# Graph attention on one core: gaps in SBUF that set how the operands of the matmuls lie modulo 256

## The reference

```python
def gat_layer(x, W, a_s, a_d, b, edge_index, concat):
    h = (x @ W).reshape(n, H, C)
    alpha_s = einsum('nhc,hc->nh', h, a_s); alpha_d = einsum('nhc,hc->nh', h, a_d)
    e = leaky_relu(alpha_s[src] + alpha_d[dst], 0.2)
    e = exp(e - segment_max(e, dst)[dst])
    alpha = e / (segment_sum(e, dst)[dst] + 1e-16)
    return segment_sum(h[src] * alpha[:, :, None], dst).reshape(n, H * C) + b
h = elu(gat_layer(x, W1, a_src1, a_dst1, b1, edges, True))       # 8 heads of 768
out = gat_layer(h, W2, a_src2, a_dst2, b2, edges, True)          # 1 head of 768
return layernorm(x + out)
```

## The kernel before

| buffer | byte of its start | modulo 256 |
|---|---|---|
| xTh, xTl | 16512, 28800 | 128 |
| W2h, W2l | 68768, 81056 | 160 |
| hh, hl | 99488, 111776 | 160 |
| oner | 138944 | 192 |
| pad2 (48 bytes, as02 follows after 64) | 139232 | 224 |
| W1h, W1l | 140864, 159296 | 64 |
| Ph, Pl | 186080, 194272 | 224 |
| ohd, ohs | 186336, 200672 | 224 |
| gh, gl | 204640, 216928 | 96 |

## Time and profile before

### The profile page before, as it was taken

How to read it: one execution, slowest core, us unless ns; L and a number is a source line. 1 busy time by engine, 2 the same in 40 slices (tenths; PEclk the granted TensorE clock), 3 DMA queues, 4 the chain that set the end, 5 groups by cost and what they waited for, 6 DMA issues and landing times.

```text
span 634.8 us, 9260 instructions
## 1 busy us (share of the span) xinstructions
PE 627.6 (99%) x3360; PEld 537.1 (85%) x3360; DVE 537.8 (85%) x976; ACT 337.5 (53%) x570; POOL 210.8 (33%) x133
## 2 busy tenths in 40 slices
PE   9999999999999999999999999999999999999996
PEld 5766667989888898989899988999898989887885
DVE  8999997989999887778696958797798869898967
ACT  7799993535625645454354635363445344534282
POOL 2000000131643834076404940384208540451230
PEclk9999999999999999999999999999999999999998
DMA  9422413116053423043302520260217130600002
GB/s 324 158 63 87 132 44 100 50 51 199 31 170 123 152 99 101 1 126 124 100 0 64 186 61 15 75 224 14 86 41 233 52 100 5 219 26 0 1 2 100
DMA packets 22173, 59.35 MB, mean 93 GB/s; under 512 B 2544, under 2 KB 2800, under 8 KB 22128
## 3 DMA queue, kind: packets, MB, share of 16 engines
q1 hardware_dynamic: 21984, 58.69, 28.6%
q10 hardware_dynamic: 144, 0.07, 0.0%
HBM read 54.03 MB, written 4.72 MB: 93 GB/s over the span
## 4 chain that ended last, share of the span: by engine, by line
PE 89%; DVE 7%; issue 1%; ACT 1%; POOL 1%; DMA 1%; ACTq 0%; DVEq 0%
PE O L1394 27%; PE O L1302 9%; PE R L1285 8%; PE R L1288 8%; PE R L1291 8%; PE R L1361 6%; PE R L1367 6%; PE R L1364 6%; DVE L L888 1%; PE O L1361 1%; PE O L1367 1%; PE O L1364 1%; PE O L1545 1%; PE O L1551 1%; PE O L1548 1%
## 5 line engine op out<-in xcount | busy, mean ns | idle before, releaser
L1199 POOL TENSOR_TENSOR W2l<-Wr,W2h 128x768 fp32r<-128x768 f32 x48 | 91.9, 1937 | 132.9 <-ACT W2h L443 132.9
L1203 POOL TENSOR_TENSOR Pl<-L,Ph 128x512 fp32r<-128x512 f32 x34 | 55.9, 1665 | 152.5 <-ACT Ph L491 152.5
L1285 PE MATMUL R<-W1h,xTh 128*128 128x384 f32 x312 | 106.0, 340 | 0.4 <-ACT h L455 0.4
L1291 PE MATMUL R<-W1h,xTl 128*128 128x384 f32 x312 | 104.8, 336 | 0.0
L1288 PE MATMUL R<-W1l,xTh 128*128 128x384 f32 x312 | 104.7, 336 | 0.0
L1193 POOL TENSOR_TENSOR W1l<-Wr,W1h 128x768 fp32r<-128x768 f32 x30 | 59.7, 2012 | 116.9 <-ACT W1h L432 116.8
L768 DVE CUSTOM_DVE_ANT_0 junk<-h,abc 128x768 bf16<-128x768 f32 x64 | 67.0, 1046 | 23.1 <-ACT h L455 21.5
L1394 PE MATMUL O<-W2h,gh 128*128 128x256 f32 (+1 forms) x384 | 78.2, 338 | 0.0
L1394 PE MATMUL O<-W2h,gl 128*128 128x256 f32 (+1 forms) x384 | 77.8, 337 | 0.0
L1394 PE MATMUL O<-W2l,gh 128*128 128x256 f32 (+1 forms) x384 | 77.2, 335 | 0.0
L1361 PE MATMUL R<-Ph,hh 128*128 128x512 f32 x168 | 66.2, 394 | 0.0
(11 more groups left out here) (204 smaller groups left out, 1180.1 us busy)
## 6 DMA issues: line engine op xcount, KB each, us to landing
Wr<-in_W SPq DMA_DIRECT2D x101, 384.0 KB, 3.6
abc<-in_as SPq DMA_DIRECT2D x9, 384.0 KB, 4.4
abc<-in_ad SPq DMA_DIRECT2D x9, 384.0 KB, 5.7
h_rows<-h SPq DMA_DIRECT2D x8, 384.0 KB, 2.3
hl<-h_rows SPq DMA_DIRECT2D x8, 384.0 KB, 5.8
xin<-in_xT SPq DMA_DIRECT2D x6, 256.0 KB, 5.3
xr<-in_x SPq DMA_DIRECT2D x1, 1536.0 KB, 7.8
out<-res SPq DMA_DIRECT2D x4, 384.0 KB, 2.3
```

Source lines behind the costliest of these rows:

```text
L1199: e.tensor_tensor(W2l[:, m % N2, :], Wr[:, n, :], W2h[:, m % N2, :].bitcast(f32), ALU.subtract).then_inc(s_w2l, 1)
L1203: e.tensor_tensor(Pl[:, t, d0:d1], L[:, t, d0:d1], Ph[:, t, d0:d1].bitcast(f32), ALU.subtract).then_inc(s_Pl, 1)
L1285: e.matmul(bank[:, 0:HALF], xTh[:, f, xs], hi[:, ws], start=f == 0, stop=False)
L1291: m = e.matmul(bank[:, 0:HALF], xTl[:, f, xs], hi[:, ws], start=False, stop=f == FT - 1)
```

## The change

The gap `pad2`, 48 bytes that take up 64 with the rounding, is removed from before `as02`, and a gap of 128 bytes with the same name is put before `asd`. Nothing else is changed: the instructions, their order and the semaphores are the same.

```diff
--- before.py
+++ after.py
@@ -109,7 +109,6 @@
         b1s = sb("b1s", [128, H * FT], f32)
         amx = sb("amx", [128, NT], f32)
         zm = sb("zm", [128, NT], f32)
-        sb("pad2", [128, 3 * NT], f32)
         as02 = sb("as02", [128, NT], f32)
         junk = sb("junk", [128, D], bf16)
 
@@ -133,6 +132,7 @@
         sb("pad", [128, 9216 - (2 * NT * D + D + N + NT * 12 + 3 * NT * 2 + 1 + 24 + D // 2)], f32, c2)
 
 
+        sb("pad2", [128, 32], f32)
         asd = sb("asd", [128, 2, 2, NT], f32)
         va = sb("va", [128, FT, 2], f32)
```

## The result

The changed kernel takes 640.66 us (median of 4 runs, 640.51 to 640.83), the kernel before beside it 636.21 (635.87 to 636.59). The ratio is 1.0068, with an interval of 1.0056 to 1.0080: slower, by 4.4 us. The forecast was 634.0, faster. The profiled execution took 640.51 us with a span of 638.7, against 636.64 and 634.8: the span grew by 3.9 us.

What follows compares the result with a forecast made beforehand. The prediction took TensorE's own matmul pace to bound the kernel. Gains of 1.2 (B) + 0.75 (A) + 0 (C) + 0.25 (D) = 2.2 us, taken from 636.27, gave 634.0 us; range 630 to 641.5.

Steps and rivals of the forecast that it cites:

- What bounds the kernel: Whole kernel: TensorE is busy 99% of the span, so its pace sets the time; fp32r excess of 40 us is the room.
- the place modulo 256: In fp32r stages: address of moving operand less weights, modulo 256; 64 was claimed to cost less than 192.
- Rival 1: All stages: the change does nothing, the excess not hanging on addresses, or effects cancel; 636.3 us, chance 0.22.
- the rule set beside it: Trainium skill on SBUF and TensorE: TensorE has own ports, two independent reads, so no place costs more; no change in time.
- B: 1.2 us less: Stage B (x by W1, 384 columns), place 192 to 128: C's 172.8 ns for 174.0, over 1008 matmuls.
- A: 0.75 us less: Stage A (h by P, 512 columns), place 64 to 128: half of a 1.5 us gain, over 576 matmuls.
- C: 0: Stage C (activations by W2, 256 and 512 columns), place 64 to 0: no change; bounds 3.5 us less, 3.0 more.
- D: 0.25 us less: Stage D (96 matmuls, 512 and 256 columns), place 192 to 128: steps from 232.5 and 118.3 to 228.9 and 116.7 ns.
- Head 1 and the other engines: 0: Head 1's 48 matmuls, at most 0.1 us either way, taken as 0; VectorE and ScalarE 0 either way.
- The low end of the range: Whole kernel: B and A at their shortest steps plus D, 4.0 + 1.5 + 0.25 less, near 630.3 us.
- the tail to 651: Upper tail of rival 2: up to 651 us were all of B, A and C to take the longest step seen.
- Rival 2: Slower because two reads meet at place 0: C 3.0 us more, A 1.0 more, B stays; 640.3 us, chance 0.36.

Runs made afterwards that it cites:

- the probe: Not a changed kernel: copies x to the output while TensorE alone runs matmul groups at chosen places, plain or in the stages' orders; steps were read, no kernel time given.
- The kernel with B alone: Against the kernel before, only W1 and what shares its room moved down 64 bytes, stage B from place 192 to 128; 637.52 us against 636.52, ratio 1.0015.
- The run with A and D alone: Against the kernel before, P (with L, y2, one-hots) moved 64 bytes modulo 256: stage A from place 64 to 128, D from 192 to 128; 638.33 us, ratio 1.0031.
- The run with C alone: Against the kernel before, only gh and gl moved up 64 bytes: stage C from place 64 to 0, head 1's B in gl 224 to 32; 637.10 us, ratio 1.0010.

## Why the prediction was wrong, by its own steps

**What bounds the kernel** held: TensorE's pace, no new wait that costs time, busy time and span up alike. So did the mechanism, the place modulo 256, which the probe shows with TensorE alone. Rival 1, and the rule set beside it, fall by the same rows: 227 to 234 ns for one shape at one clock. The Trainium skill, "TensorE: Matmul & The Clock Gate", section "Part 2: What happens when you issue a matmul", says that the next load doesn't steal read bandwidth from the running matmul. bf16 agrees (215.8 ns at every place tried); for fp32r that rule leaves no room for the steps of 227 to 234 ns, though no run shows that it is the reading that waits.

**B: 1.2 us less, in fact about 1.9 more.** The failed step is "128 can reach no farther from 192 than 64 without passing other places". It took an order of places from C, which has other widths, and a pair (A and D), and treated the place as a scale. The nearest measured value was B's own 174.0; the step at 128 is 175.9, +1.9 x 1008 = 1.9 us, inside the stated bound of 2.7 more. The kernel with B alone measured 1.0 us more: the first of B's matmuls lie ahead of 185 us, where the traces show no lag left over, and from there on B's lag is 0.9 us.

**A: 0.75 us less, in fact 2.3 more.** At 128 the step is 232.4 to 233.3 ns against 229, 4 x 576 = 2.3, just beyond the bound of 2.1, which was D's level. Half of a gain was taken because the three products differ by 5 ns at one place; that difference is one among three products in one cycle and told nothing of another place. The run with A and D alone cost 1.8 us, part of it through B, which ran at 175.0 behind A.

**C: 0, in fact 1.7 more.** The 512-column steps went from 229.3 to 232.6 ns, the 256-column ones from 116.5 to 116.1: 576 x (3.3 - 0.4) = 1.7. The run with C alone cost 0.6. "The row nearest to place 0 is 1 ns from no change" rested on seven single matmuls at a boundary between stages; that such a matmul isn't typical of a stage is argued, not shown. The bound from D, 3.0 more, held.

**D: 0.25 us less, in fact 0.1 more**: 232.2 to 233.1 and 117.3 to 118.6 ns over all its steps. **Head 1 and the other engines: 0** was right; head 1's B went from 174.7 to 174.4.

**The sum** of the measured terms is 1.9 + 2.3 + 1.7 + 0.1 = 6.0 us; 4.4 were measured. The rest is the stretch before 185 us, where no lag is left over, and 0.6 us of waiting that went. The low end of the range has a slip, 636.27 - 5.75 = 630.5 and not 630.3, and the tail to 651 has no working; neither matters here.

**Rival 2** gave 640.3 for 640.66 measured, with the right sign, by other shares: it had 3.0 in C, 1.0 in A and 0 in B. Its total fits better than its terms. What should have raised its chance was in the rows: the three other places seen with 512 columns (0, 160 and 192) had 394 to 398 ns against A's 392, so 64 was the one place known to be good there, and the change left it in both stages that stood on it.

**Still open:** why 128 is bad and why the best place hangs on the width, whether it is a read that waits and which, and what picks the pace of a stage at a place that has several. What could (the banks written, how load and stream stand to each other when the stage begins) wasn't separated.

## What to carry to other kernels

When a kernel is bound by fp32r matmuls with a load for each, the difference of the two operands' addresses modulo 256 is worth 1 to 3% of their time; measure the pace at each place, in the kernel's own order and widths, with TensorE alone, before any gap is moved. Don't rank unseen places by their distance from seen ones, and treat a place that is known to be good as something to lose. Check the stages behind the one that was moved, too: one whose addresses stay can change its pace, and where a place has several paces the probe doesn't tell which one the kernel will take. A place that showed one pace whatever ran ahead is the safer choice.

## What the runs showed of the hardware that was not expected

- fp32r with a 128 x 128 load for each matmul: 227.3 ns (place 0) to 234.2 (160) for 512 columns, 173.3 to 176.7 for 384, 117.7 to 119.8 for 256. It goes on below 32 bytes: with 512 columns place 4 took 237.1 ns, 8 233.1, 16 231.7, 48 233.3, 80 231.3.
- bf16: 215.8 ns for 512 columns, at each of three places.
- One stage at one place (B at 192) runs at 173.1, 174.6 or 176.7 ns, steadily over 54 matmuls, by what ran ahead of it; the place of the stage ahead doesn't settle which (173.1 and 174.8 behind A at 128).
- Order matters at one place: 512 columns are quickest at 0, yet C's order of 256 and 512 is slower there (174.4 on the mean) than at 64 (172.8).
